# The first layer of a graph network reads its dense input from a copy that the host has transposed

## What is computed

```python
def _sage_conv(x, src, dst, Wl, b, Wr):
    agg  = segment_sum(x[src], dst, num_segments=n)      # 50,000 edges, sorted by dst
    cnt  = segment_sum(ones, dst, num_segments=n)
    mean = agg / maximum(cnt, 1.0)[:, None]
    return mean @ Wl + b + x @ Wr

x = layernorm(x + conv_a2(relu(conv_a1(x))))
x = layernorm(x + conv_b3(relu(conv_b2(relu(conv_b1(x))))))
```

## Time and profile before

| | us |
|---|---|
| median of 3 runs | 5494.6 (5491.9 to 5495.12) |
| the profiled execution, its own time | 5473.94 |
| its span, first to last instruction | 5472.3 |
| TensorE busy in the span | 5178.4 (95%) |
| DVE, ACT, POOL busy | 3574.3, 2560.0, 2278.1 |
| first and last addition of pass a1 | 165.0, 920.1 |

### The profile page before, as it was taken

One profiled execution on the slowest core, in us unless ns is written; L12 is line 12 of the kernel. 1 busy time (PEld: TensorE's weight loads), 2 busy tenths in 40 slices (PEclk: granted clock), 3 DMA queues, 4 the chain that ended last, 5 costly groups with the idle time before them and its releaser, 6 DMA issues. The chain is left out here.

```text
span 5472.3 us, 161658 instructions
## 1 busy us (share of the span) xinstructions
PE 5178.4 (95%) x44358; PEld 5110.7 (93%) x44359; DVE 3574.3 (65%) x9610; ACT 2560.0 (47%) x7254; POOL 2278.1 (42%) x2959
## 2 busy tenths in 40 slices
PE   1999998999999899999989999999999899999999
PEld 0899998889888899999989999999999899999999
DVE  4344444777777788888866666666666455555555
ACT  0343433777777433333333333333333466666666
POOL 1665655555555344444432322322222333333332
PEclk9999999999999999999999999999999999999999
DMA  1555554666667566666655555555555566666666
GB/s 29 150 168 164 172 167 143 202 202 206 205 200 208 164 194 192 194 195 195 193 165 177 173 178 176 174 179 174 174 180 169 178 217 219 217 219 220 216 219 195
DMA packets 1322822, 1006.82 MB, mean 184 GB/s; under 512 B 70406, under 2 KB 1278627, under 8 KB 1322756
## 3 DMA queue, kind: packets, MB, share of 16 engines
q1 hardware_dynamic: 1247044, 825.23, 48.6%
q0 software_dynamic: 75712, 180.76, 10.7%
HBM read 645.58 MB, written 360.13 MB: 184 GB/s over the span
## 5 line engine op out<-in xcount | busy, mean ns | idle before, releaser
L1043 PE MATMUL f_product_b<-f_ring_b,f_onehot_b 128*128 x6272 | 996.5, 281 | 0.0
L690 PE MATMUL m_product_a<-m_ring_a,m_onehot_a 128*128 x6272 | 959.8, 276 | 0.0
L1043 PEld LDWEIGHTS f_product_b<-f_ring_b,f_onehot_b 128*128 128x128 f32 x6272 | 855.8, 188 | 0.0
L1099 ACT ACTIVATE f_ring_b<-f_e_product_b,t_rec_all 128x256 f32 (+1 forms) x784 | 328.9, 471 | 1099.1 <-PE f_e_product_b L1056 1091.1
L792 DVE TENSOR_TENSOR m_onehot_a<-iota_all,t_win_all 128x512 f32<-128x512 f32 x784 | 537.5, 686 | 454.4 <-PE m_product_a L690 388.4
L690 PEld LDWEIGHTS m_product_a<-m_ring_a,m_onehot_a 128*128 128x128 f32 x6272 | 829.5, 193 | 0.0
L1037 PE MATMUL f_product_b<-b_r_all,f_t_hi_b 128*128 128x256 f32 x2352 | 723.2, 307 | 0.0
L1039 PE MATMUL f_product_b<-b_r_all,f_t_lo_b 128*128 128x256 f32 x2352 | 661.0, 281 | 0.0
L1038 PE MATMUL f_product_b<-b_r_all,f_t_hi_b 128*128 128x256 f32 x2352 | 659.4, 280 | 0.0
L686 PE MATMUL m_product_a<-a_r_all,m_t_full_a 128*128 128x128 f32 x3136 | 608.0, 276 | 0.0
L976 POOL TENSOR_TENSOR f_held_b<-ones_all 1x1 f32<-1x1 f32 x390 | 71.4, 183 | 1236.0 <-ACT f_e_idx_b L1081 1157.1
(11 more groups left out here) (193 smaller groups left out, 12135.2 us busy)
## 6 DMA issues: line engine op xcount, KB each, us to landing
g<-f_rows_out_b SPq DMA_DIRECT2D x392, 512.0 KB
f_rows_in_b<-g SPq DMA_DIRECT2D x196, 512.0 KB
m_rows_in_b<-g SPq DMA_DIRECT2D x196, 512.0 KB
m_rows_in_a<-in_x_dram SPq DMA_DIRECT2D x196, 256.0 KB
h<-m_rows_out_a SPq DMA_DIRECT2D x196, 256.0 KB
m_rows_in_a<-h SPq DMA_DIRECT2D x196, 256.0 KB
m_res_in_a<-in_x_dram SPq DMA_DIRECT2D x196, 256.0 KB
x<-m_rows_out_a SPq DMA_DIRECT2D x196, 256.0 KB
```

The costliest lines, as they stand in the source:

```text
L690: mm = pe.matmul(to, onehot[:, s, n, :], ring[:, bass.ds(at[n] * fo, fo)], start=False, stop=(w == 1), skip_group_check=True)
L1043: mm = pe.matmul(to, onehot[:, s, n, :], ring[:, bass.ds(at[n] * (2 * fo) + half * fo, fo)], start=False, stop=(w == 1 and half == 1))
```

## The change

Each half is told for what it does in the program.

- The host passes a second input, `x_flat`, the transpose of x, [128 features, 100,000 nodes], made before the launch. In layer a1 SyncE loads the columns of a group straight into `m_t_full`: 128 pieces of 2 KB. `m_rows_in`, the bank `m_turned`, `turn_nodes` and `nodes_full` are gone from that layer.
- `m_t_full` has three buffers in a1 (R = 3). A load waits until the product that used its buffer is done (`s_product`, two groups before), where it waited for the transposes of the group before.
- The three narrow passes are driven by a new loop (`phased`, with positions written as `At`): six steps in each turn, on SyncE too; the first six and the last ten groups are written out.
- The code gains two options, `split` and `ahead`, which no layer sets: with them off, D = 2 and C = 1 as before. They are left out of the diff below. a2 and b3 do the same operations as before. The gather of a1 still reads x by rows.

```diff
+PHASES = 6
...
+class At:
+    def __init__(self, off, reg=None):
+        self.off, self.reg = off, reg
+    def n(self, more=0, times=1):
+        at = (self.off + more) * times
+        return at if self.reg is None else self.reg * (PHASES * times) + at
...
+def phased(pr, eng, step):
+    G = pr.groups
+    for p in range(LEAD):
+        step(None, At(p))
+    turns = (G - LEAD) // PHASES
+    for g in range(PHASES):
+        step(At(g), At(g + LEAD))
+    with eng.Fori(1, turns) as turn:
+        for m in range(PHASES):
+            step(At(m, turn), At(m + LEAD, turn))
+    for g in range(turns * PHASES, G - LEAD):
+        step(At(g), At(g + LEAD))
+    for g in range(G - LEAD, G):
+        step(At(g), None)
...
+    R = 3 if flat is not None else 2
...
-        rows_in = pr.sb(c, "m_rows_in", [P, 2, T, kt * P])
-        t_full = pr.sb(c, "m_t_full", [P, 2, kt, GROUP])
+        if flat is None:
+            rows_in = pr.sb(c, "m_rows_in", [P, 2, T, kt * P])
+        t_full = pr.sb(c, "m_t_full", [P, R, kt, GROUP])
...
-            def load_rows(g, s):
-                wait(sp, s_turned, (g - 1) * kt)
-                sp.dma_start(rows_in[:, s, :, :], view(h, g, kt * P)).then_inc(rows_here[s].sem, 16)
+            def load_rows(g):
+                if flat is not None:
+                    wait(sp, s_product, g.n(1 - R))
+                    sp.dma_start(t_full[:, g.slot(R), 0, :], flat[:, bass.ds(base(g), GROUP)]
+                                 ).then_inc(rows_here[g.slot(R)].sem, 16)
...
                 if u == 0:
-                    ready = g + LEAD - 2
-                    wait(pe, s_full, (g + 1) * kt)
+                    if flat is not None:
+                        wait(pe, rows_here[r], g.turn(R) + 1)
...
                 if g is not None:
                     at = places(g)
-                    if not is_last(g):
-                        turn_nodes(g + 1, 1 - s, i + s)
-                    multiply(g, s, at, 0)
+                    if not is_last(g) and flat is None:
+                        turn_nodes(g.plus(1))
+                    multiply(g, at, 0)
...
-                if g is not None and not is_last(g):
-                    nodes_full(g + 1, 1 - s)
+                if flat is None:
+                    if g is None and p.off == LEAD - 1:
+                        nodes_full(At(0))
+                    if g is not None and not is_last(g):
+                        nodes_full(g.plus(1))
...
-            dict(name="a1", h=x, out=h1, relu=False, w=1, f_out=128, turned=True, Wl=a_wl1, Wr=a_wr1, b=a_b1),
+            dict(name="a1", h=x, out=h1, relu=False, w=1, f_out=128, turned=True, flat=x_flat, Wl=a_wl1, Wr=a_wr1, b=a_b1),
...
+    arrays["in_x_flat_dram"] = _np.ascontiguousarray(_np.asarray(inputs["x"]).T)
+    args.append(nc.dram_tensor("in_x_flat_dram", shape[::-1], F32, kind="ExternalInput").ap())
```

More of the change, by code:

```diff
@@ L596, in _ @@
[L596 to L600, removed]
-                if has(g, late):
[L602 to L607, removed]
-            with sp.Fori(1, G // 2 - 2) as i:
-                for s in range(2):
-                    step(i * 2 + s, s, True)
@@ new lines, in load_res, with store @@
+            def load_res(g):
+                wait(sp, s_total, g.n(-1))
+                sp.dma_start(res_in[:, g.slot(2), :, :], view(res, g, P)).then_inc(res_here[g.slot(2)].sem, 16)
+            def store(g):
+                wait(sp, s_done, g.n(1))
+                if is_last(g):
+                    wait(sp, stored[1 - g.slot(2)], G // 2)
+                sp.dma_start(view(out, g, fo), rows_out[:, g.slot(2), :, :]).then_inc(stored[g.slot(2)].sem, 16)
+            ahead = R if flat is not None else 3
@@ new lines, in step @@
+            def step(g, p):
+                if g is None:
+                    if p.off < ahead:
+                        load_rows(p)
+                        if norm and p.off < 2:
+                            load_res(p)
+                    return
+                if g.reg is not None or g.off + ahead < G:
+                    load_rows(g.plus(ahead))
+                if has(g, late):
+                    store(g.plus(-late))
+                if norm and (g.reg is not None or g.off + 2 < G):
+                    load_res(g.plus(2))
@@ L682, in multiply @@
+                    wait(pe, s_ring, min(g.off + LEAD - 2, G) if g.reg is None else g.n(LEAD - 2))
+                    wait(pe, s_sum, g.n(-1))
+                    if norm and not split:
+                        pe.matmul(product[s][:, :], pr.two_rows[:, :],
+                                  cv["bias_row"][:, :, :].rearrange("p a n -> p (a n)"),
                                   start=True, stop=False, skip_group_check=True)
+                if split:
+                    pe.matmul(halves(s)[:, 2 * u:2 * u + 2, 0, :], pr.two_rows[:, :], cv["bias_row"][:, 0:2, :],
+                              start=True, stop=False, skip_group_check=True)
@@ new lines, in ring_low @@
+            def ring_low(p):
+                wait(v, s_ringhi, p.n(1))
+                for a in range(2):
+                    at = ((p.n(0, 2) + a) % RING) * (C * fo)
+                    ins = v.scalar_tensor_tensor(out=ring[:, bass.ds(at + fo, fo)],
+                                                 in0=e_product[:, a * fo:(a + 1) * fo],
+                                                 scalar=pr.t_rec[:, bass.ds(p.n(0, 2) + a, 1)],
+                                                 in1=ring[:, bass.ds(at, fo)].bitcast(F32),
+                                                 op0=ALU.mult, op1=ALU.subtract)
+                ins.then_inc(s_ring.sem, 1)
```

366 lines of the change are left out of this document (216 added, 150 removed).

## The result

The changed kernel takes 5439.8 us in the median (5437.1 to 5442.4, 4 runs), and the kernel before took 5494.9 beside it: a ratio of 0.9901, 95% interval 0.9887 to 0.9914. The profiled execution took 5437.1 us, with a span of 5435.5. The forecast of 5437 was met, but not by the sum behind it: that it came out is luck, as the passes show.

The account below looks back on a forecast made before the run. The prediction took TensorE as a1's bound, with gathers setting the pace in late stretches. It took 57 us for a1 off the profiled 5473.9 us, other terms at nothing, adjusted 0.4% to the median: 5437 us, range 5404 to 5476.

Parts of the forecast that it names:

- They gain 0.41 us each ... and 56 x 0: Pass a1: 140 groups gain 0.41 us each, 56 groups in late stretches gain nothing; 57 us in all.
- the round of the gather buffer: a1's two-buffer gather loop, the next limit: 6.5 us a round, to fit in 6.68 us after the change.
- 0.03 for the gathers, chosen small since the trace still leaves 0.2 us: a1, groups outside late stretches: allowance for gather jitter reaching TensorE, 0.03 us within 3.42 us a group.
- the late stretches: Two stretches of a1, 56 groups, where gathers set the pace at 3.98 us a group; expected to gain nothing.
- the second rival: a1: tighter gather round missed oftener; half late gives 5461 us, late everywhere 5516; late nearly everywhere had chance 0.03.
- No cost, with 3 us to spare: SyncE in a1: the store behind the load goes out later but still lands before DVE needs it; 0 us.
- about 96 ns: a1's dense load: estimated time of one 2 KB DMA piece, making a load 0.8 us of all engines against 0.9.
- The column slices are slow: Rival, a1's load: rows 400 KB apart cost more, deciding from 309 ns a packet; 5560 us at 350 ns; chance 0.02.
- TensorE's sequencer, 0 to 30 us: a1: fetching ring places loses 0.44 us of lead; no cost taken, 0 to 30 us if fetches show.
- taken as 0, range -10 to +10: Passes a2 and b3 through the rewritten loops: a few us either way, counted as 0.
- if a2 or b3 move by more than the whole of a1's gain: Sign that the prediction is wrong; a2, b1, b2 and b3 were expected unchanged within 10 us each.
- The profiled execution as the base: Whole kernel: 57 us off the profiled 5473.9 us, then 0.4% taken off as the gap to the median 5494.6.

Follow-up runs that it names:

- both edits: The changed kernel with a1's store issued ahead of the load and a third gather buffer in a1: 5338.5 us, ratio 0.9798 to the kernel before.
- the contiguous blocks: The changed kernel with each group's columns laid out by the host as one contiguous 256 KB block: 5434.5 us, ratio 0.9884 to the kernel before.
- the loops alone: The changed kernel with a1 put back on rows (load, transposes, copy), leaving only the rewritten loops: 5458.2 us, ratio 0.9922 to the kernel before.

## Why the prediction was right, and where it wasn't

The time and the sign came out, and TensorE's floor was right: 3.34 us a group was worked out for 30 records, and 3.34 was measured, though with both edits and not in the changed kernel. The total is luck. Its term for a1 was 41 us too large, and terms put at nothing made up for it: 20 us in a2, and 18 us by which the medians differ more than the profiled executions. By the profiled executions alone the sum gives 5473.9 - 57 = 5417, and 5437.1 was measured.

- *"They gain 0.41 us each ... and 56 x 0": 57 us for a1.* It gave 16. The transposes were worth their 0.44 us a group, as a1 with both edits shows, and the round of the gather buffer was rightly named as the next limit: taking a gather out gave 81 us, a third buffer 24, and with the store first the floor. The step that failed is "0.03 for the gathers, chosen small since the trace still leaves 0.2 us": the groups lie 3.79 us apart, not 3.42 and 3.58 in the mean. A slack of 0.2 us in a round of 6.7, with one round in five known to be 1.4 us longer, is no slack. The late answers did not stay as many as they were, but doubled. The prediction took it that the late stretches "stay as long as they are"; the counter's times show TensorE's signal late in them, and what makes it late isn't known. This is the second rival, "locks into the late rhythm", at a share of (3.79 - 3.42)/(3.98 - 3.42) = 0.66 by its own formula.
- *The store: "No cost, with 3 us to spare".* DVE waited for it 44 times, 39.0 us, and putting it first gave 22 (15 on one chip). Two things used up the 3 us: the store goes out 2.8 us behind its addition in the median, where before it went out at 0.2, since it stands behind a load that waits for the product, and it takes 3.2 us to land where DVE waits for it, not the 1.9 read from the last store of a pass, which finds the queue empty.
- *The load, "about 96 ns"* a piece: 128. The line through packets of 512 B and a 745 B mean fell a quarter short. A load takes 1.0 us of all engines, more than the 0.9 of before, not less. The DMA share came out at 0.63, as forecast, for another reason: fewer groups per time at more each. The Trainium skill, "DMA: Bandwidth & Descriptors", Specifications, holds 512 B to be enough for full rate; by these rows 2 KB pieces move 16 bytes a ns and engine and 512 B pieces (27 ns) 19, so the larger piece has no gain here either.
- *"The column slices are slow"*: a packet takes 0.128 us, far from the 309 ns that would decide, and the contiguous blocks rule the distance out.
- *TensorE's sequencer, 0 to 30 us.* In after line 772 waits for issue 25 times, 10.0 us, within the range; with both edits 0.1 us of idle is left before that line. So nothing, once the rest is even.
- *The other passes, "taken as 0, range -10 to +10".* b3 stayed to 0.1 us; a2 gave 20, ten of them with the loops alone. This is the error that hid the first one. It is also one of the prediction's own signs of being wrong ("if a2 or b3 move by more than the whole of a1's gain"): a2 gave more than a1, so by the profiles the mechanism that was forecast is not where the time came from.
- *The profiled execution as the base.* It was taken as 0.4% under the median of before, and after's is only 0.05% under its own (5437.1 against 5439.8). By profiles the gain is 37 us, by medians 55; 18 us of the median's gain are in no row shown.

## What to carry to other kernels

When work is taken from the engine that bounds a loop, compute the round of every buffer behind it and give each a full group of slack before counting the gain; here a round that fitted by 3% lost most of it, and one more small buffer, with the store put first, gave it back. On an in-order queue put what someone waits for ahead of what must itself wait. And check a forecast pass by pass: a right total can be two wrong terms.

## What the runs showed of the hardware

- ScalarE's start after TensorE's last matmul of a project step is 0.2 to 0.3 us behind its end in most groups, and over 1 us (in after up to 2.7) in 19 to 37% of them in nine profiles and in none in five. What is late is the rise of TensorE's counter, by 0.8 to 2.4 us in after; ScalarE starts within 0.25 us of it. All 65 late starts of after, all of before and 67 of 69 with three gather buffers have the second of two gathers, issued back to back, as the last that GpSimd began before them. So do 39 of the 120 starts in time of after, but 114 of 149 in before, so it is a strong sign in the one and a weak one in the other. The cause isn't known.
- The same program took 5449.5, 5475.9, 5494.9 and 5500.1 us in its medians on four occasions, three of them on different chips, while pass b3 of the changed kernels agrees to 0.2 us over all of them. Where in before the spread lies isn't shown, since it was profiled once only.
- A loop turn of two groups in place of six, on TensorE, ACT, DVE and POOL, cost 25 us in a1 (196 groups), 0.13 us a group, and 4 us in a2.
